# A graph attention layer: drains behind TensorE's groups in the edge stage, and index columns copied 32 at a time

## What is computed

```python
h = relu(layernorm(x))
q = h @ wq + bq ; k = h @ wk + bk ; v = h @ wv + bv
scores = sum(q[dst] * k[src], axis=-1) * scale + edge_weight * we + be
attn = exp(scores - segment_max(scores, dst)[dst])
attn = attn / segment_sum(attn, dst)[dst]
out = segment_sum(v[src] * attn, dst)
r = layernorm(h + out + h @ ws + bs)
result = x + layernorm(r + gelu(r @ w_ff1 + b1) @ w_ff2 + b2)
```

## Time and profile before

| | us |
|---|---|
| median of 3 runs | 2562.84 (2562.78 to 2564.1) |
| the profiled run | 2571.49 |
| span of the profiled run, first to last instruction | 2569.4 |
| TensorE busy, matmul | 2285.8 (89%) |
| GpSimd busy | 1963.4 (76%) |
| VectorE busy | 1757.6 (68%) |
| ScalarE busy | 1141.8 (44%) |

### The profile page before, as it was taken

The page is one execution under the profiler, slowest core; times in us unless marked ns, Lnnn a source line. Parts: engine busy times, 40 slices in busy tenths (PEclk is TensorE's granted clock), DMA queues, the critical chain, the costliest instruction groups (busy, mean ns, idle before and its releaser), DMA issues. The chain is left out here.

```text
span 2569.4 us, 72091 instructions
## 1 busy us (share of the span) xinstructions
PE 2285.8 (89%) x14569; PEld 1811.4 (70%) x14570; DVE 1757.6 (68%) x7421; ACT 1141.8 (44%) x2765; POOL 1963.4 (76%) x3334
## 2 busy tenths in 40 slices
PE   5978888888888889889999999999999999989994
PEld 3756666666666667667677777777777777877883
DVE  5856666666666667667676777777777777775367
ACT  2544333434444444444444444444444444455454
POOL 2148888888888888888888888888888888802355
PEclk7989999999999999999999999999999999999997
DMA  6344444444444444444444444444444444440014
GB/s 201 109 132 123 123 123 122 123 124 123 123 124 123 123 123 124 125 125 124 124 123 124 122 123 124 122 123 124 122 123 124 123 122 123 123 106 29 0 53 138
DMA packets 140341, 302.96 MB, mean 118 GB/s; under 512 B 33710, under 2 KB 76833, under 8 KB 140312
## 3 DMA queue, kind: packets, MB, share of 16 engines
q0 software_dynamic: 75264, 205.62, 28.0%
q1 hardware_dynamic: 62910, 96.62, 11.2%
q10 hardware_dynamic: 2138, 0.40, 0.1%
HBM read 282.87 MB, written 19.65 MB: 118 GB/s over the span
## 5 line engine op out<-in xcount | busy, mean ns | idle before, releaser
L787 POOL DMA_INDIRECT work<-h_rows,idx x1568 | 1527.9, 974 | 252.2 <-issue 252.2
L855 PE MATMUL bank<-work 128*128 x3520 | 837.0, 380 | 0.0
L809 PE MATMUL bank<-q,onehot 128*128 x5304 | 745.4, 275 | 99.9 <-DVE work L914 90.0
L914 DVE SCALAR_TENSOR_TENSOR work<-bank,work 128x257 bf16<-128x257 f32 x1764 | 646.2, 424 | 255.1 <-SPq L757 250.6
L855 PEld LDWEIGHTS bank<-work 128*128 128x128 f32 x3520 | 635.1, 190 | 79.1
L809 PEld LDWEIGHTS bank<-q,onehot 128*128 128x128 bf16 x5304 | 501.4, 98 | 211.2 <-issue 145.3
L876 ACT ACTIVATE work<-work 128x1 f32<-128x1 f32 x440 | 129.6, 295 | 948.7 <-DVE work L971 948.7
L880 ACT COPY work<-bank 128x256 f32<-128x256 f32 x880 | 284.6, 375 | 234.6 <-PE bank L842 233.0
L842 PE MATMUL bank<-ident,work 128*128 128x128 f32 x1760 | 286.5, 285 | 76.9 <-ACT work L877 69.0
L903 DVE TENSOR_SCALAR onehot<-dst_words,node 128x512 bf16 x443 | 168.8, 381 | 263.0 <-issue 211.2
L842 PEld LDWEIGHTS bank<-ident,work 128*128 128x128 f32 x1760 | 184.6, 140 | 232.4 <-ACT work L877 225.3
(11 more groups left out here) (182 smaller groups left out, 1511.1 us busy)
## 6 DMA issues: line engine op xcount, KB each, us to landing
dst_words<-dst_short SPq DMA_DIRECT2D x99, 512.0 KB
work<-h_rows,idx POOLq DMA_INDIRECT x1568
h_rows<-work SPq DMA_DIRECT2D x49, 128.0 KB, 1.7
r_rows<-work SPq DMA_DIRECT2D x49, 128.0 KB, 1.7
work<-r_rows SPq DMA_DIRECT2D x49, 128.0 KB, 2.1
acc<-in_x SPq DMA_DIRECT2D x4, 1536.0 KB, 15.6
work<-in_x SPq DMA_DIRECT2D x48, 128.0 KB, 2.2
out<-work SPq DMA_DIRECT2D x48, 128.0 KB, 1.9
```

The lines of the kernel that those rows point to most:

```text
L787: pool.indirect_dma_start(rows[:, u, j, 0:D], None, h_rows, bass.IndirectOffsetOnAxis(idx[:, u * J + j:u * J + j + 1], 0)).then_inc(rows_i ...
L809: last = nc.tensor.matmul(banks[j][:, 0:D1], onehot[:, k, j, :], q3[:, bass.ds(b, 1), c, 0:D1], start=(c == 0), stop=(c == 2))
L855: last = nc.tensor.matmul(banks[6 + k][:, 0:D1], probs[:, j, :], rows[:, bass.ds(slot, 1), j, :], start=(j == 2), stop=(j == 1))
L914: last = nc.vector.scalar_tensor_tensor(out=product[:, j, 0:D1], in0=banks[j][:, 0:D1], scalar=SCALE, in1=rows[:, bass.ds(slot, 1), j, :], ...
```

## The change

On TensorE, in the edge stage, no matmul or transpose carries an increment any more. Behind each of the groups stands a `drain`, and behind that an increment made by the sequencer. The two increments of `turned`, one behind each pair of transposes, become one of two, behind all four. On GpSimd the copy of one column behind each gather goes. `idx` gets two halves of 32 columns, and in each window of eight chunks, ahead of the last chunk, one copy of 32 columns fills the other half. `idx_set` counts windows instead of chunks. The windows are unrolled by two, and at the end of a round GpSimd waits until all chunks have landed before it copies the first window's columns again.

```diff
-        idx = sb("idx", [P, G * J], I32)
+        idx = sb("idx", [P, 2, G * J], I32)
...
-                g.tensor_copy(idx[:, 0:LEAD * J], idx_all[:, 0:LEAD * J]).then_inc(idx_set, LEAD)
+                g.tensor_copy(idx[:, 0, :], idx_all[:, 0:G * J]).then_inc(idx_set, 1)
...
-                def gather(first, u, next_first):
+                def gather(first, half, u):
                     chunk = pool.to_reg(first + (u + 1))
                     pool.wait_ge(dst_out, 2 * 16)
                     pool.wait_ge(slot_free, chunk)
+                    for j in range(J):
+                        pool.indirect_dma_start(rows[:, u, j, 0:D], None, h_rows, bass.IndirectOffsetOnAxis(idx[:, half, u * J + j:u * J + j + 1], 0)).then_inc(rows_in[u][j], 16)
+
+                def next_idx(half, first):
+                    nc.gpsimd.tensor_copy(idx[:, half, :], idx_all[:, first]).then_inc(idx_set, 1)
+
+                with pool.Fori(0, rounds) as r:
+                    with pool.Fori(0, NW // 2) as i:
+                        for half in range(2):
+                            first = pool.snap(pool.to_reg(r * TP + i * (2 * G) + half * G), min_val=0, max_val=B * TP)
+                            ready = pool.to_reg(r * NW + i * 2 + (half + 1))
+                            pool.wait_ge(dst_out, 2 * 16)
+                            pool.wait_ge(idx_set, ready)
+                            for u in range(G):
+                                gather(first, half, u)
+                                if u == G - 2:
+                                    next_idx(1 - half, bass.ds(i * (2 * G * J) + (half + 1) * G * J, G * J))
...
+                    pool.wait_ge(chunk_landed, all_landed)
+                    next_idx(0, slice(0, G * J))
...
-                            last = nc.tensor.matmul(banks[j][:, 0:D1], onehot[:, k, j, :], q3[:, bass.ds(b, 1), c, 0:D1], start=(c == 0), stop=(c == 2))
-                    last.then_inc(q_edges, 1)
+                            nc.tensor.matmul(banks[j][:, 0:D1], onehot[:, k, j, :], q3[:, bass.ds(b, 1), c, 0:D1], start=(c == 0), stop=(c == 2))
+                    pe.drain()
+                    pe.sem_inc(q_edges, 1)
...
-                    last.then_inc(spread, 1)
+                    pe.drain()
+                    pe.sem_inc(spread, 1)
...
-                            last.then_inc(turned, 1)
+                        pe.drain()
+                        pe.sem_inc(turned, 2)
...
-                        last.then_inc(summed, 1)
+                        pe.drain()
+                        pe.sem_inc(summed, 1)
```

More of the change, by code:

```diff
@@ L783, in gather @@
                     pool.wait_ge(slot_free, chunk)
-                    pool.wait_ge(dst_out, 2 * 16)
[L785 to L797, removed]
+                    for j in range(J):
+                        pool.indirect_dma_start(rows[:, u, j, 0:D], None, h_rows, bass.IndirectOffsetOnAxis(idx[:, half, u * J + j:u * J + j + 1], 0)).then_inc(rows_in[u][j], 16)
@@ new lines, in next_idx @@
+                def next_idx(half, first):
[11 more added lines that the diff above has]
+                                    next_idx(1 - half, bass.ds(i * (2 * G * J) + (half + 1) * G * J, G * J))
+                    first = pool.snap(pool.to_reg(r * TP + (NW - 1) * G), min_val=0, max_val=B * TP)
+                    ready, all_landed = pool.to_reg(r * NW + NW), pool.to_reg(r * TP + TP)
+                    pool.wait_ge(dst_out, 2 * 16)
+                    pool.wait_ge(idx_set, ready)
@@ L798, in _ @@
                     for u in range(G):
-                        gather(first, u, lambda j: slice((((NW - 1) * G + u + LEAD) % TP) * J + j, (((NW - 1) * G + u + LEAD) % TP) * J + j + 1))
+                        gather(first, 0, u)
+                    pool.wait_ge(dst_out, 2 * 16)
+                    pool.wait_ge(chunk_landed, all_landed)
+                    next_idx(0, slice(0, G * J))
             @block.tensor
@@ L808, in expand_q @@
                         for c in range(3):
-                            last = nc.tensor.matmul(banks[j][:, 0:D1], onehot[:, k, j, :], q3[:, bass.ds(b, 1), c, 0:D1], start=(c == 0), stop=(c == 2))
-                    last.then_inc(q_edges, 1)
+                            nc.tensor.matmul(banks[j][:, 0:D1], onehot[:, k, j, :], q3[:, bass.ds(b, 1), c, 0:D1], start=(c == 0), stop=(c == 2))
+                    pe.drain()
+                    pe.sem_inc(q_edges, 1)
                 def spread_scores(k):
                     for j in range(J):
-                        last = nc.tensor.transpose(banks[4][:, j * P:(j + 1) * P], score[:, k, j:j + 1].broadcast_to([P, P]), ident[:])
-                    last.then_inc(spread, 1)
+                        nc.tensor.transpose(banks[4][:, j * P:(j + 1) * P], score[:, k, j:j + 1].broadcast_to([P, P]), ident[:])
+                    pe.drain()
+                    pe.sem_inc(spread, 1)
                 pe.load(regs[0:2], steps_tab[0:1, 0:2])
@@ L841, in trip @@
                             for j in range(2):
-                                last = nc.tensor.transpose(banks[5 - half][:, j * P:(j + 1) * P], probsT[:, (2 * half + j) * P:(2 * half + j + 1) * P], ident[:])
-                            last.then_inc(turned, 1)
+                                nc.tensor.transpose(banks[5 - half][:, j * P:(j + 1) * P], probsT[:, (2 * half + j) * P:(2 * half + j + 1) * P], ident[:])
+                        pe.drain()
+                        pe.sem_inc(turned, 2)
                         pe.wait_ge(onehot_done, s + (S + 3))
@@ L854, in trip @@
                                 pe.wait_ge(probs_done, s * 2 + 2)
-                            last = nc.tensor.matmul(banks[6 + k][:, 0:D1], probs[:, j, :], rows[:, bass.ds(slot, 1), j, :], start=(j == 2), stop=(j == 1))
-                        last.then_inc(summed, 1)
+                            nc.tensor.matmul(banks[6 + k][:, 0:D1], probs[:, j, :], rows[:, bass.ds(slot, 1), j, :], start=(j == 2), stop=(j == 1))
+                        pe.drain()
+                        pe.sem_inc(summed, 1)
                 trips(pe, trip)
```

## The result

| | kernel before | kernel after |
|---|---|---|
| median | 2563.47 us (2562.78 to 2570.06, 4 runs) | 3804.49 us (3768.58 to 3825.76, 4 runs) |
| profiled run, its span | 2571.49, 2569.4 | 3768.58, 3766.8 |
| granted TensorE clock over the span | 0.982 | 0.925 |
| starts of the maxima, first to last | 183.6 to 2265.0 | 181.7 to 3458.2 |
| a step, mean | 4.74 | 7.46 |

The ratio is 1.4786, with a 95% interval of 1.4666 to 1.4906: 48% slower, where 37% (3510 us) was forecast, in a range of 3220 to 3820. One of the four runs after, the 3825.76, was a slow one: the ratio leaves it out, and the median of the other three is 3792.29. The whole difference lies in the edge stage: 3458.2 - 181.7 = 3276.5 us between the first and the last maximum against 2081.4, and 490 us outside these against 488.

What follows compares the result with a forecast made beforehand. Gathers on GpSimd were taken to bound the kernel, TensorE 0.6 us a step behind. With drains, 5.17 + 1.5 + 0.24 = 6.9 us a step; 439 x 6.9 + 488 = 3517, so 3510 us, range 3220 to 3820.

Steps and rivals of the forecast that it cites:

- Lengths of the groups: TensorE groups on an idle array: transposes 0.65, q halves 0.86 and 0.83, spread 0.65, sum 1.90 us; with drains 5.17.
- Twelve register instructions of 0.1 us: TensorE's register instructions in each step run behind drains instead of beside matmuls: 1.2 us a step.
- The drain itself: Each TensorE drain ends 0.05 us after the last matmul, and the next instruction follows 0.06 us later.
- The trip's head: Once in 8 steps TensorE loads step words and branches: about 1.9 us beyond an ordinary head, 0.24 a step.
- no gap above 0.7: Argument against the clock falling: TensorE busy some 4.9 of 6.9 us a step, with no longer gap.
- the granted clock still 1.00: Sign expected in the profile: TensorE's granted clock stays at 1.00, that is 2.4 GHz.
- The clock: Rival, 4%: more gaps on TensorE make its clock fall to half, giving 4560 to 5220 us.
- a step of 7.45: Slow end of the main case: sem_inc's on TensorE are instructions of their own, 0.53 us a step more.
- the 66 us for the drains alone: Allowance at the ends of the range: 0.03 us more or less for each drain on TensorE.
- The pitch of the gathers: GpSimd's gathers without copies between them start 0.975 to 1.13 us apart; 1.13 was taken.
- the gathers win: Rival, 7%: drains hardly hold TensorE's sequencer, its step stays 4.1 us, and the run takes about 2290 us.
- 440 fed steps: Edge stage if removing the index copies alone ended all starvation of VectorE: some 1790 us.

Runs made afterwards that it cites:

- x_regs2: Kernel after, with the five register instructions for the next step moved ahead of the sum's drain in seven of eight steps: 3563.09 us, ratio 1.3897 to the kernel before.
- x_index: Kernel before with only the GpSimd part of the change, one copy of 32 index columns per 8 chunks, no drains: 2457.67 us, ratio 0.9586.
- x_head: Kernel after without the sum's drain in the last step of each trip of eight, the increment on its last matmul: 3556.07 us, ratio 1.3856.

## Why the prediction was right, and where it was off

The mechanism was the one forecast: the drain holds TensorE's sequencer until the last matmul is done, groups no longer overlap, the register work is laid bare, and the faster gathers buy nothing. The size was 8% low. By the steps of the prediction, for an ordinary step, from each group's start to the next one's:

| | predicted: group and drain, registers | measured |
|---|---|---|
| transposes | 0.71 + 0.36 = 1.07 | 1.08 |
| q, first half | 0.92 + 0.26 = 1.18 | 1.17 |
| spread | 0.71 + 0.16 = 0.87 | 0.86 |
| q, second half | 0.88 + 0.16 = 1.04 | 1.08 |
| sum | 1.95 + 0.56 = 2.51 | 2.61 |
| step | 6.67 | 6.80 |

- **Lengths of the groups**: four of five hold to 0.05 us. The sum was taken from the earlier trace rows, 1.90, where it starts while q is still running; on an idle array it is 2.00. That is 0.10 of the 0.13 us in the table; the rest is the gap ahead of the sum, 0.24 instead of 0.21. With the rounding of the forecast's step to 6.9 it makes 0.14 a step, 61 us.
- **Twelve register instructions of 0.1 us**: right by the gaps, and x_regs2 shows it for five of them.
- **The drain itself**: forecast as 0.05 us to its end and 0.06 to the next instruction; measured 0.02 and 0.10. The sum is right. The increment is carried by the drain, as taken: the step with the increments elsewhere is shorter by 0.05 us, not by 0.53.
- **The trip's head**: 1.9 us beyond an ordinary one was forecast, 1.96 measured. But it was spread over eight steps as 0.24, and the argument on the clock then spoke of "no gap above 0.7". By the prediction's own terms the head's gap is 0.6 + 1.9 = 2.5 us in one piece. **This is the step that failed**, and with it the sign "the granted clock still 1.00".
- **The clock**: put down as a rival with 4%, priced as if it fell for the whole stage (4560 us and more). It fell for part of each trip, 473 us together, which cost 3.3 us a trip, 55 x 3.3 = 181 us. The case between never and always was not among the rivals. The repeated runs spread in step with the granted clock: 3768.6 us at 0.925, 3792.3 at 0.916, 3816.7 at 0.912, against 7 us of spread before.
- The sum with what was measured: 3517 + 61 + 181 + 2 for the rest of the program = 3761, against a profiled span of 3766.8. The median lies another 36 us above the profiled run. That the time still lies in the range is luck in part: the upper end came from a step of 7.45, with the increments as instructions of their own, which they are not. By the step of 6.9 and the 66 us for the drains alone the end would have been 3576, and the clock's 181 us had no place in it.
- **VectorE, ScalarE, SyncE**: as forecast. The maximum waits for the drain (L827), the gathers for slot_free (L761), the landed rows for nobody (10.8 us). The single increment of turned shows as ScalarE's wait for L855 and delays nothing that TensorE needs in time: TensorE has no wait of size but issue.
- **The index copies**: the copy of 32 columns took 0.22 us in the median, inside the bound of 0.4. The pitch of the gathers was bounded at 0.975 to 1.13 and is 1.25, outside it. The upper end assumed that the idle time ahead of a gather is the same with a copy ahead as with a gather ahead; it is 0.15 in the one case and 0.30 in the other. It did no harm to the forecast, because the gathers were hidden in either case. It would have in the rival "the gathers win": with drains for nothing the time would have been x_index's 2458, not 2290. So the loop's first bound, the gathers, was also misjudged: without their copies they need 1968 us, not the some 1790 of 440 fed steps.

## What to carry over

An increment on the last matmul lets the sequencer run ahead; a drain gives that up. Its price is the lost overlap plus all register work that follows, so it is read from the sequencer's lines, not from the drain's own, and work moved from behind it to ahead of it is won back. When a cost that comes once per trip is averaged into a sum, keep its undivided length too: all 54 gaps of 2.58 us were followed by half clock here, and an eighth of such a gap, added to each step, shows nothing of that. And an engine's idle time ahead of an instruction depends on what stands before it, so a copy of 0.19 us between two gathers may be worth only 0.08.

## What the runs showed of the hardware

- A drain ended 0.02 us after the last matmul, and the next instruction on TensorE's sequencer started 0.10 us later. With one register instruction between, a group's first matmul came 0.21 to 0.24 us after the one before it, with five 0.62.
- A gap of 2.58 us at a trip's head, with the other groups laid apart too, was followed by a granted clock of 0.50 at all 54 heads that have it; with a gap of 0.96 at 19 of 54; with a gap of 2.59 to 2.64 but overlapped groups there were 24 falls in 55 trips.
- 331 us fewer at half clock went with 125 us less time, the shorter gaps taken off (x_head against the kernel after).
- Gathers on GpSimd, each of 128 rows, start no closer than 1.24 us although each lasts 0.95.
- Eight fp32 matmuls took 2.00 us on an idle array, and 1.90 behind other matmuls.
